# Moving small steps of a two-part transformer block: another order at the seams, other engines and other queues

## The reference

```python
mod = silu(c) @ wmod                       # 4 x 768
n1 = layernorm(x) * (1 + scale1) + shift1
h  = two attention layers on n1            # rmsnorm, rope, 16 heads of 8; causal, then a window of 32
x  = x + gate1 * h
n2 = layernorm(x) * (1 + scale2) + shift2
f  = two local-attention layers on n2      # 8 heads of 64, windows of 64, each with a gated MLP of 341
x  = x + gate2 * f
```

## Time and profile before

| | us |
|---|---|
| median of 3 runs | 1239.72 (1236.19 to 2293.99) |
| profiled execution, device time | 1240.99 |
| its span | 1239.1 |
| busy in it: TensorE | 1120.7 (90%) |
| VectorE | 957.8 (77%) |
| ScalarE | 822.6 (66%) |
| GpSimd | 381.4 (31%) |

### The profile page before, as it was taken

The page is one execution under the profiler, slowest core; times in us unless marked ns, Lnnn a source line. Parts: engine busy times, 40 slices in busy tenths (PEclk is TensorE's granted clock), DMA queues, the critical chain, the costliest instruction groups (busy, mean ns, idle before and its releaser), DMA issues.

```text
span 1239.1 us, 37488 instructions
## 1 busy us (share of the span) xinstructions
PE 1120.7 (90%) x16048; PEld 696.0 (56%) x16048; DVE 957.8 (77%) x1524; ACT 822.6 (66%) x1207; POOL 381.4 (31%) x538
## 2 busy tenths in 40 slices
PE   4488889899889999688999999999999999999987
PEld 3133434344445667455666666666666666666654
DVE  7969693969668688886887788778878877877865
ACT  3498898989888876345655665665566566655644
POOL 1203220202200014665533433343333333323420
PEclk8599999999999999789999999999999999999999
DMA  3113130122113541110211111111111111110102
GB/s 109 34 23 127 50 107 20 34 86 103 34 67 103 171 153 54 52 26 20 75 28 23 28 28 23 28 28 24 23 24 24 27 24 27 27 24 19 33 10 69
DMA packets 41684, 61.71 MB, mean 50 GB/s; under 512 B 7440, under 2 KB 16816, under 8 KB 41520
## 3 DMA queue, kind: packets, MB, share of 16 engines
q1 hardware_dynamic: 39728, 58.44, 16.2%
q10 hardware_dynamic: 1792, 0.87, 0.3%
HBM read 22.61 MB, written 16.78 MB: 32 GB/s over the span
## 4 chain that ended last, share of the span: by engine, by line
PE 52%; DVE 3%; ACT 3%; issue 1%; DVEq 0%; ACTq 0%
PE psum L1392 9%; PE psum L1536 7%; PE psum L1481 6%; PE psum L1503 5%; PE psum L1467 4%; PE psum L1402 4%; PE psum L1412 4%; PE psum L1562 3%; PE psum L1489 2%; PE psum L1424 2%; PE psum L1452 2%; ACT ffn_probs L1770 2%; PE psum L1432 1%; PE psum L1458 1%; PE psum L1527 1%
## 5 line engine op out<-in xcount | busy, mean ns | idle before, releaser
L865 ACT ACTIVATE att_probs<-psum 128x1024 f32<-128x1024 f32 x352 | 334.9, 1028 | 39.3 <-PE psum L723 39.2
L1910 POOL TENSOR_TENSOR ffn_rot<-ffn_rot,ffn_rot_sin 128x512 f32<-128x512 f32 x128 | 160.1, 1272 | 378.5 <-DVE ffn_rot L1945 378.5
L764 PE MATMUL psum<-att_probs,att_v 128*32 128x256 f32 (+3 forms) x3072 | 178.6, 347 | 3.7 <-DVE att_probs L1058 3.1
L723 PE MATMUL psum<-att_q_stack,att_k_parts 64*128 64x512 bf16 (+2 forms) x1472 | 132.9, 273 | 43.2 <-ACT att_probs L865 32.1
L723 PEld LDWEIGHTS psum<-att_q_stack,att_k_parts 64*128 64x128 bf16 x1472 | 45.3, 94 | 143.5 <-ACT att_probs L865 105.3
L1763 ACT ACTIVATE ffn_max_t<-psum 68x128 bf16<-68x128 bf16 x64 | 17.5, 273 | 157.6 <-PE psum L1440 157.4
L764 PEld LDWEIGHTS psum<-att_probs,att_v 128*32 128x32 f32 x3072 | 79.8, 110 | 62.1 <-issue 37.7
L1058 DVE TENSOR_TENSOR att_probs<-att_probs,att_causal_mask 128x1024 f32<-128x1024 f32 (+1 forms) x80 | 94.7, 1199 | 25.7 <-ACT att_probs L865 25.5
L1770 ACT ACTIVATE ffn_probs<-psum 128x1024 f32<-128x1024 f32 x64 | 65.6, 1025 | 56.3 <-PE psum L1467 56.3
L1732 ACT ACTIVATE ffn_sq<-psum 128x512 f32<-128x512 f32 x128 | 74.6, 595 | 23.0 <-PE psum L1392 22.0
L1481 PEld LDWEIGHTS psum<-ffn_v_back,ffn_probs 128*64 128x64 f32 x1024 | 64.9, 138 | 31.9 <-ACT ffn_probs L1770 17.9
(11 more groups left out here) (237 smaller groups left out, 2396.4 us busy)
## 6 DMA issues: line engine op xcount, KB each, us to landing
ffn_v_back<-ffn_v SPq DMA_DIRECT2D x120, 130.0 KB, 2.4
att_q_stack<-q_rows SPq DMA_DIRECT2D x28, 512.0 KB, 3.7
q_rows<-att_q_high SPq DMA_DIRECT2D x21, 256.0 KB, 2.6
q_rows<-att_q_mid SPq DMA_DIRECT2D x21, 256.0 KB, 2.7
q_rows<-att_q_low SPq DMA_DIRECT2D x14, 256.0 KB, 4.1
xres<-in_hidden SPq DMA_DIRECT2D x4, 512.0 KB, 5.9
out<-ffn_qk_t SPq DMA_DIRECT2D x3, 512.0 KB, 3.3
tail_f_wqkv<-in_f_wqkv SPq DMA_DIRECT2D x1, 768.0 KB, 4.6
```

Source lines behind the costliest of these rows:

```text
L723: ins = T.matmul(psum[:, banks[i] + at:banks[i] + at + width], k_parts[rows, p % 3, j, key:key + P], q_stack[rows, turn % 2, j, q0:q0 + wi ...
L764: ins = T.matmul(psum[32 * g:32 * g + V_PAD, (4 + cc) * BANK + lo - cc * BANK: (4 + cc) * BANK + hi - cc * BANK], v_of(p, kt, g, shift), p ...
L865: act.activation(probs[:, n % E_BUFS, 2 * j:2 * j + 2, 0:width], ps2((step % 2) * 2).rearrange("p (h c) -> p h c", h=2)[:, :, 0:width], AC ...
L1910: steps.did(pool.tensor_tensor(out, out, halves(k.rot_sin[:, n % 2, :])[:, :, 1 - half, :], ALU.add), g["added"] if half else None)
```

## The change

It has five groups of edits. (1) The rows of phase 0 are evacuated by ScalarE, in the tick of their transposes. (2) GpSimd does the modulation, ahead of its first tick, in other operations. (3) ScalarE's eight gathers of turn 0 are shared: three high ones by ScalarE as soon as its own copy is done, three middle ones by GpSimd, two low ones by ScalarE. (4) At the seam of the halves: other ticks for the steps of `POST_STEPS`; the scale and shift of batch 1 goes to GpSimd's period 2 of the second half; GpSimd's gated addition of batch 2 goes from ahead of period 0 to period 1; `make_bands` and `tail_copy_sums` go from VectorE to ScalarE. (5) The scalings go from the periods 47, 55, 63 to 50, 58, and half each to 63 and 64, and stand ahead of the maxima's copy; write-out 0 goes into period 65, write-out 1 ahead of the last up-products, 2 between them and 3 behind, with other banks and waits to suit.

```diff
-FIRST = dict(square=0, transpose=0, reduce=0, evacuate=1, ...
+FIRST = dict(square=0, transpose=0, reduce=0, evacuate=0, ...
-POST_STEPS = (dict(gate=0, stats=2, roots=4, norm=4, shift=6, transpose=10, evacuate=10),
-              dict(gate=0, stats=2, roots=4, norm=5, shift=6))
-MODULATE_AT = -10
+POST_STEPS = (dict(gate=0, stats=1, roots=2, norm=3, shift=4, transpose=10, evacuate=10),
+              dict(gate=0, stats=3, roots=5, norm=6))
-SUMS_ON_ACT, HEADS_ON_ACT, ROWS_ON_ACT = 8, 3, 6
+SUMS_ON_ACT, HEADS_ON_ACT, ROWS_ON_ACT = 8, 3, (0, 6, 7)
...
         @block.gpsimd
         def _(pool):
...
+            def modulate():
+                for b in range(1, B):
+                    c.did(pool.tensor_scalar(scales[:, b], scales[:, b], 1.0, None, ALU.add))
+                c.did(pool.tensor_scalar(gate_tmp, gates, 0.0, 2.0, ALU.is_ge, ALU.mult))
+                c.settle()
+                c.did(pool.tensor_scalar(gate_tmp, gate_tmp, -1.0, None, ALU.add))
+                c.settle()
+                c.did(pool.tensor_tensor(gates, gate_tmp, gates, ALU.mult))
+                c.settle()
+                c.did(pool.tensor_scalar(gates, gates, 0.25, None, ALU.max))
+                c.settle()
+                c.did(pool.tensor_tensor(gates, gate_tmp, gates, ALU.mult))
+                c.settle()
+                c.did(pool.tensor_copy(keep.gate_b[:], mod[:, :, 5 * D:6 * D]), mod_ready)
+
+            modulate()
             for n in range(FIRST_TICK, LAST_TICK):
+                if n == FIRST_GATHER_AT:
+                    pool.wait_ge(q_split_ready, 1)
+                    for term in range(PARTS, 2 * PARTS):
+                        gather(pool, 0, 1, term, gathered_mid)
...
                     c.did(act.activation(q_parts[0][:, p % 2], side, ACT.Copy), hi_ready)
+                    if p == 0:
+                        act.wait_ge(hi_ready, 1)
+                        for term in range(PARTS):
+                            gather(act, 0, 1, term, gathered[0])
...
                 if n == FIRST_GATHER_AT:
-                    act.wait_ge(hi_ready, 1)
-                    for term in range(TERMS):
-                        if term in (PARTS, 2 * PARTS):
-                            act.wait_ge(q_split_ready, term // PARTS)
-                        gather(act, 0, 1, term)
+                    act.wait_ge(q_split_ready, 2)
+                    for term in range(2 * PARTS, TERMS):
+                        gather(act, 0, 1, term, gathered[0])
...
-                if n == MODULATE_AT:
-                    modulate()
...
-SCALE_AT = (47, 55, 63)
+SCALE_AT = {50: (0, 0, 2), 58: (1, 0, 2), 63: (2, 0, 1), 64: (2, 1, 2)}
...
-    OUT_BANKS = (4, 0, 2, 4)
+    OUT_BANKS = (2, 4, 2, 0)
-    LAST_UP_BANKS = {(0, 0): 3, (1, 0): 0, (2, 0): 1, (0, 1): 7, (1, 1): 4, (2, 1): 5}
+    LAST_UP_BANKS = {(0, 0): 7, (1, 0): 0, (2, 0): 1, (0, 1): 4, (1, 1): 5, (2, 1): 7}
...
             def tail_transposes(b, half):
-                if b > 1 and half == 0:
-                    pe.wait_ge(g["tail_n_ready"], b - 1)
+                if half == 0:
+                    pe.wait_ge(g["tail_n_ready"], b)
...
             def last_up(j, part):
                 if j == 0 and part == 0:
                     pe.wait_ge(g["hn_ready"], LAST + 1)
+                    pe.wait_ge(g["y_added"], LAST)
                 if j == 0 and part == 1:
-                    pe.wait_ge(g["y_added"], LAST)
-                if j == 1 and part == 1:
-                    pe.wait_ge(g["out_gated"], 1)
+                    pe.wait_ge(g["out_gated"], 2)
+                if j == 2 and part == 1:
+                    pe.wait_ge(g["gelu_ready"], ALL_BLOCKS * LAST + 1)
...
                     project_out(n - 3)
+                if n == STREAM + 1:
+                    write_out(0)
...
             xn_transposes(LAST)
-            write_out(0)
-            for part in range(2):
-                for j in range(ALL_BLOCKS):
-                    last_up(j, part)
-            for i in range(1, 4):
-                write_out(i)
+            write_out(1)
+            for j in range(ALL_BLOCKS):
+                last_up(j, 0)
+            write_out(2)
+            for j in range(ALL_BLOCKS):
+                last_up(j, 1)
+            write_out(3)
...
                 if live(n):
                     head_roots(n)
+                if n == 0:
+                    make_bands()
+                if n in SCALE_AT:
+                    scale_rows(*SCALE_AT[n])
...
-            gated_add(pool, steps, tail, keep, 2, g["tail_gated"])
-            steps.settle()
-            pool.memset(keep.xs[:, 2, 0:1], 0.0).then_inc(g["tail_edge"], 1)
             for n in range(STREAM):
+                if n == 1:
+                    gated_add(pool, steps, tail, keep, 2, g["tail_gated"])
+                    steps.settle()
+                    pool.memset(keep.xs[:, 2, 0:1], 0.0).then_inc(g["tail_edge"], 1)
+                if n == 2:
+                    scaled_and_shifted(pool, steps, tail, x_rows[1], 1, 4, 3, g["tail_n_ready"])
...
             gate(LAST - 1, 1)
...
             finish(LAST - 1)
-            write_out(0)
+            write_out(1)
+            write_out(2)
             for j in range(ALL_BLOCKS):
                 gate(LAST, j)
-            for i in range(1, 4):
-                write_out(i)
+            write_out(3)
             write_last()
```

102 lines of the change are left out of this document (46 added, 56 removed).

## The result

The changed kernel takes 1224.07 us (median of 4, 1219.61 to 1225.7), the kernel before 1239.64 beside it. The ratio is 0.988, 95% interval 0.986 to 0.991. So a change of 1.2% is clear here, against the prediction's remark that one within 2% can hardly be told from none. The profiled execution took 1225.7 us with a span of 1223.9, 15.2 less than the span of before.

A forecast was written before the change was run, and what follows sets the result against it. TensorE bounds the second half's long middle, so only its waits can be gained. Start -1.3, attention's end -3.0, first periods -2.7, scalings -3.9, end -4.6 sum to -15.5: 1225.5 us profiled, 1224.2 against the median; range 1215 to 1233.

The forecast's parts named there:

- the signs that it named: First scores 1-2 us earlier; no TensorE shift wait; 42.37 us periods; no 3.3 us end wait; last store <3 us.
- Start, first part: Before the first scores: ScalarE evacuates rows, GpSimd modulates; cosine product 1.0 us later, bounds 2.1 earlier to 2.5 later.
- Rival 1: Start and first periods: GpSimd's lock costs more, VectorE's tiny operations wait for products; total -9.5, 1230 us; chance 0.15.
- Start, second part: Gathers before the first scores issued on three queues instead of ScalarE's eight in a row: 2.3 us gained.
- Attention: Turns 5 to 165 of attention, not edited: 0 us.
- Rival 4: Unedited attention turns: VectorE's masks newly meet GpSimd's passes, up to 2.34 us each; slower than before, 1248 us; chance 0.04.
- End of attention: Last attention turns: batch 0's shift and the bank come free earlier, so TensorE's transposes start sooner; -3.0 us, bounds -4.0 to -1.0.
- the two links that it named: End of attention: GpSimd's shift of batch 0 (to 492.68) and the bank held by VectorE's normalised sums (to 492.04).
- First periods: Start of second half: casts leave VectorE, gated passes no longer precede GpSimd's first rope sum; -2.7 us, bounds -4.0 and 0.
- Scalings: Periods 47 and 55: scalings move into ScalarE's 6.00 us idle before the maxima; 1.93 us each, -3.9, bounds -4.6 and -2.0.
- End: From period 63: scaling -3.5, write-out +0.65, fewer last transposes -0.5, spread stores -1.3; sum -4.6 us, bounds -7.0 and -2.0.
- Rivals 2 and 3: 2: only ScalarE's three scaling places pay, 1233 us, chance 0.06; 3: warm seams and start gain more, 1214 us, chance 0.11.

The follow-up runs named there:

- the passes alone: Changed kernel with passes of GpSimd, alone and then beside VectorE's work, added behind the last store; no whole time given, as the added time is the passes' own.
- The split modulation: Changed kernel with seven modulation operations on VectorE in its idle time, the rest on GpSimd behind the cosine product; 1219.55 us, ratio 0.985.

## Why the prediction was right, and where a step was not

The time was 1224.07 us where 1224.2 was forecast. Of the signs that it named, the first was missed: the first scores came 0.1 us earlier, not 1 to 2. The others came as named. By its steps:

- **Start, first part (+1.0).** The step that failed is the sum of 9.9 us for GpSimd's passes: it took the length of one pass of 544 columns, two operations to bf16, for passes of other operations to float32. The passes took 19.7. The rule "one small operation of VectorE gets in per pass of GpSimd" was right for products and wrong in its place: the tiny steps before 22 us lost 0.8 in all, those from 30 us on 3.3. By the runs the evacuation on ScalarE brings 0.8 (2.9 from the kernel before to the one with the modulation on VectorE, less 2.1 for the queues; the cosine product comes 0.78 earlier between the two; no run has this edit by itself) and GpSimd's modulation costs 2.8: together +2.0 in place of +1.0. The scatter of one program at the first exponentials, 1.7 us, is as large as such differences, so they hold by the single steps and not by the sum. Rival 1's mechanism is thus in the trace. It did not decide, since it stands in one place and not at the seam.
- **Start, second part (-2.3).** Right: 2.1 measured alone. The net of both parts was 0.1 in place of 1.3.
- **Attention (0).** The 1.5 us there are nothing that the change does: the kernels that are the changed one there needed between 0.7 less and 1.6 more for the same stretch. The 1.6 are those of the passes alone, lost by 123 us, with a granted clock of 0.60 from 55 to 63 and 0.57 from 119 to 127 us where the changed kernel had 0.68 and 0.79. In the kernel before it was another thing, TensorE stood still within a group of value products:

```profile
415.96 0.62 PE L764 MATMUL psum<-att_probs,att_v_moved 128*32 128x96 f32 x20 [1.07 <-issue]
```

  It waited there for nothing that the profile shows. The split modulation loses 0.7 us near the same instructions, the other kernels nothing there. What it is stays open. Rival 4's new meetings of masks did not come in the middle of attention. Two came at its end, masks of 2.6 and 2.9 us at 478.8 and 484.4 in the new order of the seam (none there in the old one), and the seam brought its 2.9 in spite of them.
- **End of attention (-3.0).** Right, 2.9. Of the two links that it named, the bank was needed by its run; the shift bounds in the old order by its trace, 0.6 us behind the bank.
- **First periods (-2.7).** 2.1 measured. In period 1 both of its terms were needed, VectorE's relief and GpSimd's earlier rope sum, since undoing either costs 2.4 there; in period 7 only VectorE's relief is left, 2.3 by its run.
- **Scalings (-3.9).** Right, 4.0, and ScalarE's wait took them as computed.
- **End (-4.6).** 4.5: 3.7 for the third scaling (3.5 predicted, clock and all), 0.7 lost by the write-outs (0.15 predicted: those that I thought to save behind the last up-products were paid between them), 1.5 won at the stores (1.3).

That the total fits to 0.2 us is partly luck: the start brought 1.2 less than forecast, and the 1.5 in attention, which the change did not make, filled it up. Rivals 2 and 3 fall by the seam's runs and by the low bounds that were not reached.

The larger luck is the clock. Granted clock from 498 to 590 us, of the changed kernel and then of the kernel with scalings 0 and 1 back, which is the same program there:

```profile
498.00:590.00 92.00, 76.63 (x975) 51.23 (x976) 71.90 (x141) 47.60 (x96) 61.63 (x78) 0.89 0.19 51
```

```profile
498.00:590.00 92.00, 74.74 (x1058) 51.28 (x1058) 75.46 (x145) 48.61 (x99) 63.24 (x72) 0.94 0.20 55
```

Over the profiles that are the changed kernel in this stretch, the way from 454.8 to period 7 was 0 to 0.4 us shorter than in the first profile at 0.89, 0.4 and 0.9 at 0.91, 3.0 at 0.93 (the passes alone), and 2.1 and 3.8 at 0.94. The same projection of four matmuls over 512 columns took 3.37 us in one and 1.88 in the other:

```profile
568.41 3.37 PE L1398 MATMUL psum<-tail_f_wqkv,xs 128*128 128x512 f32 x4
```

```profile
564.26 1.88 PE L1399 MATMUL psum<-tail_f_wqkv,xs 128*128 128x512 f32 x4
```

With this, the seam's old order, which seemed to win 0.7 over that way, costs some 2.3 (3.0 less 0.7; 1.4 to 3.1 by the two profiles at 0.94), which agrees with the 2.15 read at the seam itself. The kernel before had 0.87, so up to a microsecond of the 2.1 in period 7 may be the clock's; the 2.65 in period 1 are not the scatter of one program, which was 0.02 there.

## What to carry to other kernels

Price a pass from a row of the same operations, type and number of inputs; the width alone misled by a factor of two to three. Before work is given to GpSimd, list which of VectorE's steps run beside it: products there hold VectorE's products until they end, and VectorE's hold GpSimd's, while reductions pass, so put a reduction beside a product. Where an engine idles ahead of a step in one part of a regular schedule, work moved there was free to a few hundredths; at both seams of this kernel two links ended together, and freeing one alone showed nothing. Where the clock varies from run to run, compare an edit with several profiles of the same program, at the first instruction behind it.

## What the runs showed of the hardware

- GpSimd's pass with one constant operation over 1024 columns of float32 is slower than its product of two tensors (2.79 and 2.34 us alone), and one with a comparison and a multiplication slower still (3.64, or 3.6 ns a column). A pass with two operations to bf16 took 0.64 us for 544 columns (1.2 ns a column), and a multiplication and addition to float32 0.32 for 160 (2.0). Which of operations, type and width decides is not shown.
- Such a constant pass holds VectorE's product up once, by 0.7 us, and not for its length; VectorE's constant passes of 0.43 us were held twice, by 0.8 each, beside one.
- Products of GpSimd and VectorE hold each other up: VectorE's 0.69 became 2.71 us, and GpSimd's 2.34 became 3.53 and 3.32 where VectorE's had begun first.
- The same wait of TensorE is followed by either clock: 2.85 us at the seam by 1.72 or 1.07 us for eight transposes. The prologue's projections, 16 matmuls of one shape, took 2.87, 4.3 to 4.6, 5.05 or 5.49 us. The Trainium skill (TensorE: Matmul & The Clock Gate, section Part 1: The HAM clock gate) calls the start at the low clock variable from run to run. One program came to its first exponentials within 1.7 us here, and in its first periods within 3.8.
